# Three ring buffers instead of two for the halves of turned keys and queries, with separate counts for their transfers

## The chip, the cores and the metric

The kernel runs on one core of one Trainium2 chip. The metric is the device time of one execution in microseconds. Before the change three runs gave 3314.86, 3321.76 and 3323.79 us; the median is 3321.76 us.

## What is computed

The reference is one transformer layer, all in 32-bit floats, on x of shape (2, 2048, 256):

```python
q, k, v = x @ Wq, x @ Wk, x @ Wv              # 16 heads of 64
q, k = rmsnorm(q, q_rms_w), rmsnorm(k, k_rms_w)
gate = softplus(einsum("bthd,hd->bht", k, u_n) / 8)
bias = -max(i - j, 0) * omega_eff[h] * gate[b, h, i]
attn = softmax(causal(q @ k.T / 8 + bias))
x = layernorm(x + (attn @ v) @ Wproj)
h = silu(w1(x)) * w2(x); h = gelu(h1(h)); h = gelu(h2(h))
x = layernorm(x + w3(h))
```

## The kernel before, in words

The program has three stages on the same core: attention (to about 2170 us of the span), the first part of the feed-forward block, and the second. The change touches attention alone. To keep the precision of 32-bit floats with the matmul's rounded type, every operand is held as a rounded half ("hi") and a rest half ("lo").

Attention goes through 32 heads (2 batches of 16), in 16 pairs. One pair is projected at once (`project`, L984), its squares are made on POOL into `sq` (L637) and summed on DVE (L826). A head's score work consists of 40 units of 128 keys by up to 512 queries: PE makes the scores (L1027, L1028, and L1030 on the diagonal), ACT takes the exponential twice (rounded `e_hi` L716, full `e_all` L723), POOL makes the rest `e_lo` (L457), and PE multiplies by the values (L1045, L1050, L1052, L1061). Ahead of that, in a separate pass for the next head, PE makes the scores once in rounded form (`max`, L1008, two banks `ps_m`) and DVE takes their maxima (L907, L910), from which a shift row per block of queries comes.

The order of the work is one list written out by hand. `attention_steps` gives each extra step (load, project, turn, max, ...) a due time in units of heads and sorts them between the units of the head that is being scored. Every engine, and SP, which issues all transfers, walks the same list and takes the steps that concern it, so that each engine's queue is in the order of the list. A head n of a pair has its four turns near the end of the head before (even n) or shortly after the start of the head before it (odd n).

A turn (`turn`, n, qb; running number i = 4n + qb) is the step that the change is about. For 512 tokens:

- PE transposes keys and queries into a bank (L995), ACT copies the bank, scaled and rounded, into `kq_hi` (L700), DVE subtracts to get `kq_lo` (L896). Each of the two is a ring of two buffers, [128, 512].
- SP issues five transfers of 128 KB out of them, since the two halves of the 128 rows have to go to rows 0 to 63 of other tiles: `kq_hi` to `k_ext` (L506) and to `q_max` (L507), both counted by `hi_dup`; `kq_hi` to `k_split` (L511), counted by `lo_dup`; `kq_lo` to `k_split` (L513) and to `q_ext` (L514), counted by `lo_dup` too. In a head's first turn the transfer of its bias rows from DRAM (L510, `rows_in`) stands between L507 and L511.
- `turned` is the wait for `hi_dup`; PE takes it before the first `max` of each block of queries and before the first scores of a block, and SP before it doubles the queries (`twice`, L523). PE waits for `rows_in` before a head's first `max`. `lo_dup` is waited for before the first scores.

The waits before a buffer is overwritten are these (ACT, L696 to L699):

```python
if i >= 2:
    act.wait_ge(hi_dup[i % 2], 32 * (i // 2))
    act.wait_ge(lo_dup[i % 2], 48 * (i // 2))
    act.wait_ge(tr_free, i - 1)
```

So ACT may not copy turn i before all five transfers of turn i - 2 have landed, the last one (L514) among them, and the exponentials behind it on ACT's queue stand still.

Pair 8 begins the second batch, so x is turned anew between heads 14 and 15: eight transfers of 256 KB into the two `x_rows` tiles (L481), eight sets of transposes (L971).

Of the kernel before, what the change touches and what calls it, by code (L numbers as in the profile page):

```python
# [12 lines left out]
H, D = 16, 64  # L13
HID = 1024
P = 128
# [30 lines left out]
IDENT_MADE = 2  # L46
GP_CONSTANTS = 8 + H + 5 + 14
E_RING, HI_RING, LO_RING, Q_RING = 3, 4, 3, 3
HT = TT // 2
# [44 lines left out]
class Kept:  # L94
# [3 lines left out]
    def __init__(self, nc, ctx):  # L98
# [3 lines left out]
        def room(*uses):  # L102
# [16 lines left out]
        self.w3_hi, self.w3_lo, self.dn_x, self.dn_y = last  # L119
        (self.wp_in,), (self.silu, self.prod), (self.dn_gelu,), (self.sq,) = room(  # L120
            [("wp_in", [P, OC, C], F32)],
# [132 lines left out]
def attention(nc, x, wq, wk, wv, q_rms_w, k_rms_w, omega, u, yt_dram, recip_dram, rows_dram, kept, w1_w, w2_w, wproj):  # L254
    ctx = ExitStack()
    with ctx:
# [20 lines left out]
        v_full = [sb(f"v_full{i}", [P, NQB, TQ // 2, VCOLS]) for i in range(2)]  # L277
        x_rows = [sb(f"x_rows{i}", [P, 2, C]) for i in range(2)]
        k_split = [sb(f"k_split{i}", [P, T], F32R) for i in range(2)]
# [16 lines left out]
        bias_out = sb("bias_out", [P, P])  # L296
        kq_hi = [sb(f"kq_hi{i}", [P, QB], F32R) for i in range(2)]
        kq_lo = [sb(f"kq_lo{i}", [P, QB], F32R) for i in range(2)]
        maxes = sb("maxes", [P, TT, NQB])
# [55 lines left out]
        qk_hi = sem("qk_hi")  # L355
        hi_dup = [sem(f"hi_dup{i}") for i in range(2)]
        lo_dup = [sem(f"lo_dup{i}") for i in range(2)]
        rows_out = sem("rows_out")
# [40 lines left out]
        def turned(eng, n, qb):  # L399

            i = NTURN * n + qb
            eng.wait_ge(hi_dup[i % 2], 32 * (i // 2 + 1))

# [59 lines left out]
        def _(sp):  # L463
# [5 lines left out]
            for step in steps:  # L469
                if step[0] == "x in":  # L470
                    b, j = step[1:]
                    if b == 0:
                        rows = slice(j * T // 2, (j + 1) * T // 2)
# [27 lines left out]
                if step[0] == "turn":  # L501
                    n, qb = step[1:]
                    s, i = n % 2, NTURN * n + qb
                    cols = slice(qb * QB, (qb + 1) * QB)
                    sp.wait_ge(qk_hi, i + 1)
                    sp.dma_start(k_ext[s][0:D, cols].bitcast(F32), kq_hi[i % 2][0:D, :].bitcast(F32)).then_inc(hi_dup[i % 2], 16)  # L506
                    sp.dma_start(q_max[s][0:D, cols].bitcast(F32), kq_hi[i % 2][D:P, :].bitcast(F32)).then_inc(hi_dup[i % 2], 16)  # L507
                    if qb == 0:
                        sp.wait_ge(rows_out, 16 * (P // SQ) * (n // 2 + 1))
                        sp.dma_start(k_ext[s][R_BIAS:R_BIAS + NBIAS, :].bitcast(F32), rows_dram[:, s * TT:(s + 1) * TT, :, :].rearrange("c r a j -> c (r a j)")).then_inc(rows_in[s], 16)  # L510
                    sp.dma_start(k_split[s][0:D, cols].bitcast(F32), kq_hi[i % 2][0:D, :].bitcast(F32)).then_inc(lo_dup[i % 2], 16)  # L511
                    sp.wait_ge(tr_free, i + 1)
                    sp.dma_start(k_split[s][D:P, cols].bitcast(F32), kq_lo[i % 2][0:D, :].bitcast(F32)).then_inc(lo_dup[i % 2], 16)  # L513
                    sp.dma_start(q_ext[s][0:D, cols].bitcast(F32), kq_lo[i % 2][D:P, :].bitcast(F32)).then_inc(lo_dup[i % 2], 16)  # L514
                if step[0] == "twice":
# [58 lines left out]
        def _(gp):  # L574
# [42 lines left out]
            for step in steps:  # L617
# [11 lines left out]
                if step[0] == "square":  # L629
# [3 lines left out]
                    if p == 0 and i == 0:  # L633
                        gp.wait_ge(s_const, 1)
                    if p or i >= 4:
                        gp.wait_ge(ss_done, 8 * p + i - 3)
# [24 lines left out]
        def _(act):  # L661
# [6 lines left out]
            for step in steps:  # L668
# [23 lines left out]
                if step[0] == "turn":  # L692
                    n, qb = step[1:]
                    i = NTURN * n + qb
                    act.wait_ge(tr_full, i + 1)
                    if i >= 2:  # L696
                        act.wait_ge(hi_dup[i % 2], 32 * (i // 2))
                        act.wait_ge(lo_dup[i % 2], 48 * (i // 2))
                        act.wait_ge(tr_free, i - 1)  # L699
                    nc.scalar.activation(kq_hi[i % 2][:], work_bank(step)[:], ACT.Copy, scale=qk_w[:, 0:1]).then_inc(qk_hi, 1)  # L700
                if step[0] == "scores":
# [24 lines left out]
        def _(dve):  # L726
# [70 lines left out]
            for step in steps:  # L797
# [92 lines left out]
                if step[0] == "turn":  # L890
                    n, qb = step[1:]
                    i = NTURN * n + qb
                    dve.wait_ge(qk_hi, i + 1)
                    if i >= 2:
                        dve.wait_ge(lo_dup[i % 2], 48 * (i // 2))
                    nc.vector.scalar_tensor_tensor(kq_lo[i % 2][:], work_bank(step)[:], qk_w[:, 0:1], kq_hi[i % 2][:].bitcast(F32),  # L896
                                                   ALU.mult, ALU.subtract).then_inc(tr_free, 1)
# [51 lines left out]
        def _(pe):  # L949
            pe.wait_ge(s_cg, IDENT_MADE)  # L950

            for step in steps:
# [57 lines left out]
                if step[0] == "scores":  # L1010
# [6 lines left out]
                    if kt == 0:  # L1017
                        turned(pe, n, qb)
                        pe.wait_ge(lo_dup[grp % 2], 48 * (grp // 2 + 1))
                        pe.wait_ge(q_dup[grp % Q_RING], 32 * (grp // Q_RING + 1))  # L1020
                        pe.wait_ge(row_in[grp % 2], 16 * (P // SQ) * (grp // 2 + 1))
# [777 lines left out]
```

## Time and profile before

| | |
|---|---|
| runs | 3321.76, 3323.79, 3314.86 us |
| profiled execution, its own time | 3318.82 us |
| its span | 3317.0 us |
| mean granted clock of TensorE | 0.979 of full speed |
| PE busy | 3136.1 us, 95% of the span |
| ACT busy | 1792.3 us, 54% |
| DVE busy | 1669.2 us, 50% |
| POOL busy | 1491.5 us, 45% |

An engine's share is the union of its instructions' times over the span of 3317.0 us. SP executes no arithmetic: what counts for it is when each transfer is issued (rows of engine SPq), and a row's time there is how long the issue held the queue, not how long the data took. In the rows of a timeline the first column is the start in us from the span's start, the second the duration in us; `x4` means four instructions merged into one row; a bracket at the end gives how long the engine had been idle and what ended that.

### The profile page before, as it was taken

The numbers are of one execution on the slowest core, as the hardware profiler recorded it, in microseconds if no ns is written. First come the engines' busy times: TensorE is split into PE (matmuls) and PEld (weight loads), VectorE is DVE, ScalarE is ACT, GpSimd is POOL, SyncE is SP. The second block draws the span as 40 slices with busy tenths as digits, with TensorE's granted clock in tenths as the row PEclk, the third lists the DMA queues.
The fourth block names the chain that finished last, engine by engine and source line by source line (L and its number), as shares of the span: only waits on it lengthen the run. The fifth ranks groups of instructions, "written<-read, shape, count | busy, mean of one in ns | idle before, by whom it ended". The sixth has DMA issues, their size and how long they took to land. (4 is left out here: it accounts for less than half of the span.)

```text
span 3317.0 us, 45968 instructions
## 1 busy us (share of the span) xinstructions
PE 3136.1 (95%) x15472; PEld 2443.5 (74%) x15472; DVE 1669.2 (50%) x3928; ACT 1792.3 (54%) x3057; POOL 1491.5 (45%) x1306
## 2 busy tenths in 40 slices
PE   3899999999999999999999999989999999999998
PEld 3667767677677676676776776768888888788887
DVE  6566566565655665656556656463322222232323
ACT  1477677676766666666667766753333322322222
POOL 4476666666665666666667666621111110000000
PEclk7899999999999999999999999989999999999999
DMA  2332422422423224224233144432233333111110
GB/s 73 71 80 46 92 63 57 96 63 53 101 50 93 61 59 95 63 52 100 47 73 80 44 94 105 108 86 90 92 97 98 96 98 119 59 67 48 57 58 20
DMA packets 196523, 249.12 MB, mean 75 GB/s; under 512 B 67264, under 2 KB 95040, under 8 KB 196160
## 3 DMA queue, kind: packets, MB, share of 16 engines
q1 hardware_dynamic: 196288, 246.19, 28.9%
q8 instruction: 123, 2.02, 0.3%
q14 instruction: 112, 0.92, 0.1%
HBM read 84.86 MB, written 43.52 MB: 39 GB/s over the span
## 5 line engine op out<-in xcount | busy, mean ns | idle before, releaser
L457 POOL TENSOR_TENSOR e_lo<-e_all,e_hi 128x512 fp32r<-128x512 f32 (+1 forms) x832 | 1034.0, 1251 | 658.6 <-ACT e_all L723 590.9
L723 ACT ACTIVATE e_all<-ps_s,bias 128x512 f32<-128x512 f32 (+3 forms) x1280 | 787.4, 622 | 168.9 <-PE ps_s L1030 78.0
L910 DVE TENSOR_REDUCE maxes<-ps_m 128x1 f32<-128x512 f32 x768 | 521.3, 686 | 372.1 <-PE ps_m L1008 369.3
L716 ACT ACTIVATE e_hi<-ps_s,bias 128x512 fp32r<-128x512 f32 (+1 forms) x832 | 559.0, 672 | 228.4 <-PE ps_s L1028 133.0
L1008 PE MATMUL ps_m<-k_ext,q_max 128*128 128x512 f32 (+3 forms) x1280 | 462.7, 383 | 54.2 <-DVE maxes L910 25.0
L1027 PE MATMUL ps_s<-q_twice,k_split 128*128 128x512 f32 (+3 forms) x1280 | 477.7, 373 | 31.5 <-ACT e_all L723 26.5
L1028 PE MATMUL ps_s<-q_ext,k_ext 128*128 128x512 f32 (+3 forms) x1280 | 470.4, 368 | 0.0
L1061 PE MATMUL ps_v<-e_lo,v_main 128*66 128x512 f32 (+1 forms) x832 | 431.9, 519 | 17.2 <-POOL e_lo L457 17.2
L1008 PEld LDWEIGHTS ps_m<-k_ext,q_max 128*128 128x128 f32 x1280 | 245.7, 192 | 203.2 <-DVE maxes L910 60.2
L907 DVE CUSTOM_DVE_ANT_0 ps_m<-ps_m,mask_row 128x128 f32<-128x128 f32 (+3 forms) x512 | 252.6, 496 | 283.6 <-PE ps_m L1008 283.4
L1045 PE MATMUL ps_v<-e_all,v_full 128*66 128x512 f32 (+2 forms) x896 | 322.7, 442 | 0.0
L1050 PE MATMUL ps_v<-e_hi,v_main 128*66 128x512 f32 (+1 forms) x832 | 322.4, 387 | 0.0
L1052 PE MATMUL ps_v<-e_hi,v_rest 128*66 128x512 f32 (+1 forms) x832 | 320.9, 386 | 0.0
L1027 PEld LDWEIGHTS ps_s<-q_twice,k_split 128*128 128x128 f32 x1280 | 243.2, 190 | 99.2 <-issue 44.2
L1028 PEld LDWEIGHTS ps_s<-q_ext,k_ext 128*128 128x128 f32 x1280 | 243.2, 190 | 32.3
L1265 POOL TENSOR_TENSOR y_in<-y_in,r_in 128x512 f32<-128x512 f32 x56 | 75.2, 1343 | 377.1 <-DMA r_in<-recip_sums 377.1
L1642 ACT ACTIVATE dn_gelu<-dn_h,dn_scale 128x512 f32<-128x512 f32 x64 | 44.1, 689 | 321.9 <-PE dn_h L1740 321.9
L1611 POOL TENSOR_TENSOR dn_rs<-dn_rs,dn_power 128x4 f32<-128x4 f32 x8 | 8.1, 1007 | 462.2 <-DVE dn_rs L1702 462.2
L1061 PEld LDWEIGHTS ps_v<-e_lo,v_main 128*66 128x66 f32 x832 | 114.9, 138 | 126.1 <-issue 50.6
L1325 ACT ACTIVATE gelu<-up_h,up_scale 128x512 f32<-128x512 f32 x64 | 44.0, 688 | 296.7 <-PE up_h L1492 296.7
L1740 PE MATMUL dn_h<-a_lo,h_hi 128*128 128x512 f32 x512 | 204.3, 399 | 0.0
L1740 PE MATMUL dn_h<-a_hi,h_lo 128*128 128x512 f32 x512 | 204.1, 399 | 0.0
(245 smaller groups left out, 6074.6 us busy)
## 6 DMA issues: line engine op xcount, KB each, us to landing
q_twice<-q_max SPq DMA_DIRECT2D x256, 128.0 KB, 2.3
yt<-y_out SPq DMA_DIRECT2D x128, 130.0 KB
k_ext<-kq_hi SPq DMA_DIRECT2D x128, 128.0 KB, 2.3
q_max<-kq_hi SPq DMA_DIRECT2D x128, 128.0 KB, 2.4
k_split<-kq_hi SPq DMA_DIRECT2D x128, 128.0 KB, 2.4
k_split<-kq_lo SPq DMA_DIRECT2D x128, 128.0 KB, 2.4
q_ext<-kq_lo SPq DMA_DIRECT2D x128, 128.0 KB, 2.4
hidden<-gelu SPq DMA_DIRECT2D x64, 256.0 KB, 2.0
```

Source lines behind the costliest of these rows:

```text
L457: on.tensor_tensor(e_lo[:, i % LO_RING, off:QB], e_all[:, u_ % E_RING, off:QB], e_hi[:, i % HI_RING, off:QB].bitcast(F32), ALU.subtract).t ...
L716: nc.scalar.activation(e_hi[:, i % HI_RING, off:QB], ps_s[u_ % 2][:, off:QB], ACT.Exp, bias=by).then_inc(hi_done, 1)
L723: nc.scalar.activation(e_all[:, u_ % E_RING, off:QB], ps_s[u_ % 2][:, off:QB], ACT.Exp, bias=by).then_inc(ex_done, 1)
L910: nc.vector.tensor_reduce(maxes[:, qt, kc:kc + 1], ps_m[m % 2][:, 0:width], AX.X, ALU.max).then_inc(mx_free, 1)
L1008: nc.tensor.matmul(ps_m[m % 2][:, 0:width], q_max[s][:, qt * P:(qt + 1) * P], k_ext[s][:, kc * QB:kc * QB + width], start=True, stop=True) ...
L1027: nc.tensor.matmul(out, k_split[s][:, k], q_twice[grp % Q_RING][:, off:QB], start=True, stop=False)
L1028: last = nc.tensor.matmul(out, k_ext[s][:, k], q_ext[s][:, q], start=False, stop=not diag)
L1045: nc.tensor.matmul(bank[0:VCOLS, off:QB], v_full[s][:, kt // TQ, kt % TQ - TQ // 2, :], e_all[:, u_ % E_RING, off:QB], start=False, stop=k ...
L1050: nc.tensor.matmul(bank[0:VCOLS, off:QB], v_main[s][:, kt, :], e_hi[:, i % HI_RING, off:QB], start=kt == 0, stop=False, skip_group_check=True)
L1052: nc.tensor.matmul(bank[0:VCOLS, off:QB], v_rest[s][:, kt, :], e_hi[:, i % HI_RING, off:QB], start=False, stop=False, skip_group_check=Tru ...
L1061: nc.tensor.matmul(ps_v[(n * NQB + qb) % 2][0:VCOLS, off:QB], v_main[s][:, kt, :], e_lo[:, i % LO_RING, off:QB], start=False, stop=kt - TQ ...
L1740: last = nc.tensor.matmul(ps_h[o % 2][:], w[:, k, col], p[:, k, :], start=k == 0 and j == 0, stop=k == OC - 1 and j == 2)
```

## The change

- `kq_hi` and `kq_lo` become rings of three.
- The `kq_hi` to `k_split` transfer moves in SP's queue from behind the bias rows to before them, and is counted by `hi_dup`, which now goes up by 48 a turn; `lo_dup` goes up by 32.
- ACT waits for `hi_dup` and `tr_free` of turn i - 3 and no longer for `lo_dup`; DVE waits for `lo_dup` of turn i - 3. `turned` waits for three transfers.
- `x_rows` takes the room of `sq`, with a wait on SP before the first `x_rows` transfer of batch 1 (sums of pair 7 taken) and one on POOL before the first square of pair 8 (x turned).

```diff
+KQ_RING = 3
-        (self.wp_in,), (self.silu, self.prod), (self.dn_gelu,), (self.sq,) = room(
+        self.x_rows, (self.wp_in,), (self.silu, self.prod), (self.dn_gelu,), (self.sq,) = room(
+            [(f"x_rows{i}", [P, 2, C], F32) for i in range(2)],
...
-        x_rows = [sb(f"x_rows{i}", [P, 2, C]) for i in range(2)]
+        x_rows = kept.x_rows
...
-        kq_hi = [sb(f"kq_hi{i}", [P, QB], F32R) for i in range(2)]
-        kq_lo = [sb(f"kq_lo{i}", [P, QB], F32R) for i in range(2)]
+        kq_hi = [sb(f"kq_hi{i}", [P, QB], F32R) for i in range(KQ_RING)]
+        kq_lo = [sb(f"kq_lo{i}", [P, QB], F32R) for i in range(KQ_RING)]
...
         def turned(eng, n, qb):
             i = NTURN * n + qb
-            eng.wait_ge(hi_dup[i % 2], 32 * (i // 2 + 1))
+            eng.wait_ge(hi_dup[i % KQ_RING], 48 * (i // KQ_RING + 1))
...
                     b, j = step[1:]
+                    if b == 1 and j == 0:
+                        sp.wait_ge(ss_done, 8 * PAIRS // B)
...
                     sp.wait_ge(qk_hi, i + 1)
-                    sp.dma_start(k_ext..., kq_hi[i % 2][0:D, :]...).then_inc(hi_dup[i % 2], 16)
-                    sp.dma_start(q_max..., kq_hi[i % 2][D:P, :]...).then_inc(hi_dup[i % 2], 16)
+                    sp.dma_start(k_ext..., kq_hi[i % KQ_RING][0:D, :]...).then_inc(hi_dup[i % KQ_RING], 16)
+                    sp.dma_start(q_max..., kq_hi[i % KQ_RING][D:P, :]...).then_inc(hi_dup[i % KQ_RING], 16)
+                    sp.dma_start(k_split[s][0:D, cols]..., kq_hi[i % KQ_RING][0:D, :]...).then_inc(hi_dup[i % KQ_RING], 16)
                     if qb == 0:
                         sp.wait_ge(rows_out, 16 * (P // SQ) * (n // 2 + 1))
                         sp.dma_start(k_ext[s][R_BIAS:R_BIAS + NBIAS, :]..., rows_dram...).then_inc(rows_in[s], 16)
-                    sp.dma_start(k_split[s][0:D, cols]..., kq_hi[i % 2][0:D, :]...).then_inc(lo_dup[i % 2], 16)
                     sp.wait_ge(tr_free, i + 1)
...
+                    if p == PAIRS // B and i == 0:
+                        gp.wait_ge(xt_full, B * NXT)
...
-                    if i >= 2:
-                        act.wait_ge(hi_dup[i % 2], 32 * (i // 2))
-                        act.wait_ge(lo_dup[i % 2], 48 * (i // 2))
-                        act.wait_ge(tr_free, i - 1)
+                    if i >= KQ_RING:
+                        act.wait_ge(hi_dup[i % KQ_RING], 48 * (i // KQ_RING))
+                        act.wait_ge(tr_free, i - KQ_RING + 1)
...
-                    if i >= 2:
-                        dve.wait_ge(lo_dup[i % 2], 48 * (i // 2))
+                    if i >= KQ_RING:
+                        dve.wait_ge(lo_dup[i % KQ_RING], 32 * (i // KQ_RING))
...
-                        pe.wait_ge(lo_dup[grp % 2], 48 * (grp // 2 + 1))
+                        pe.wait_ge(lo_dup[grp % KQ_RING], 32 * (grp // KQ_RING + 1))
```

## Rows read from the trace of the kernel before

**Rows 1.** The page, busy time of the engines, in us.

```profile
PE   3136.1 (95%) x15472; PEld 2443.5 (74%) x15472; DVE 1669.2 (50%) x3928; ACT 1792.3 (54%) x3057; POOL 1491.5 (45%) x1306
```

**Rows 2.** PE's waits, 160 to 2170 us: total us, times, longest us.

```profile
PE ps_s L1027 <- ACT e_all L723: 26.5, 14, 2.7
...
PE ps_m L1008 <- issue: 13.8, 10, 2.1
PE ps_m L1008 <- DMA q_max<-kq_hi: 8.6, 8, 3.5
PE ps_t L971 <- DMA x_rows<-in_L_attn_x_dram: 3.3, 1, 3.3
```

**Rows 3.** Line L700, what ACT's idle time before it waited for: us, times.

```profile
  DMA q_ext<-kq_lo: 78.6, 33
```

**Rows 4.** Timeline, turns of head 16, all engines; the first two turns' transfers.

```profile
1121.90 0.60 SPq L507 DMA_DIRECT2D q_max<-kq_hi  x1
...
1122.55 0.48 SPq L510 DMA_DIRECT2D k_ext<-bias_rows  x1
...
1123.07 0.47 SPq L511 DMA_DIRECT2D k_split<-kq_hi  x1
...
1125.41 0.30 PE L1008 MATMUL ps_m<-k_ext,q_max 128*128 128x128 f32 x1 [1.40 <-issue]
...
1126.76 0.69 ACT L700 ACTIVATE kq_hi<-ps_t,qk_w 128x512 fp32r<-128x512 f32 x1 [1.79 <-DMA q_ext<-kq_lo]
...
1128.72 0.60 SPq L511 DMA_DIRECT2D k_split<-kq_hi  x1
...
1130.00 0.60 SPq L514 DMA_DIRECT2D q_ext<-kq_lo  x1
...
1130.71 0.39 PE L1008 MATMUL ps_m<-k_ext,q_max 128*128 128x512 f32 x1
```

**Rows 5.** The same timeline, fourth turn of head 16 and after it.

```profile
1129.28 0.60 PE L995 MATMUL ps_p<-ident,raw 128*128 128x128 f32 x4
...
1131.93 0.60 SPq L511 DMA_DIRECT2D k_split<-kq_hi  x1
...
1132.54 0.69 ACT L700 ACTIVATE kq_hi<-ps_p,qk_w 128x512 fp32r<-128x512 f32 x1 [3.00 <-DMA q_ext<-kq_lo]
...
1133.74 0.47 PE L1027 MATMUL ps_s<-q_twice,k_split 128*128 128x512 f32 x1 [1.93 <-ACT e_all L723]
```

**Rows 6.** Line L511, from issue to landing, 120 transfers, 160 to 2170 us.

```profile
DMA to landing us min/median/max: 2.3/2.4/5.5
```

**Rows 7.** Timeline of ACT, fourth turn of head 17, an odd one.

```profile
1171.88 0.69 ACT L700 ACTIVATE kq_hi<-ps_p,qk_w 128x512 fp32r<-128x512 f32 x1
```

**Rows 8.** Timeline of PE, third block of maxima of head 16.

```profile
1140.23 0.39 PE L1008 MATMUL ps_m<-k_ext,q_max 128*128 128x512 f32 x1
```

**Rows 9.** Timeline of the start, turns of head 0.

```profile
75.88 0.45 PE L1008 MATMUL ps_m<-k_ext,q_max 128*128 128x128 f32 x1 [4.71 <-DMA k_ext<-bias_rows]
...
83.81 0.75 DVE L896 SCALAR_TENSOR_TENSOR kq_lo<-ps_p,qk_w,kq_hi 128x512 fp32r<-128x512 f32 x1 [2.56 <-ACT kq_hi L700]
```

**Rows 10.** Timeline, x of the second batch, second set of transposes.

```profile
1000.18 0.59 SPq L481 DMA_DIRECT2D x_rows<-in_L_attn_x_dram  x1
...
1003.29 1.12 PE L971 MATMUL ps_t<-ident,x_rows 128*128 128x128 f32 x4 [3.31 <-DMA x_rows<-in_L_attn_x_dram]
```

**Rows 11.** Line L637, squares of pair 7, then of pair 8: duration ns, first and last start us.

```profile
L637 POOL TENSOR_TENSOR sq<-raw x8: 1037/1040/1043, 928.1 to 954.6; 128x512 f32<-128x512 f32 x8
...
L637 POOL TENSOR_TENSOR sq<-raw x8: 1032/1040/1043, 1068.1 to 1094.4; 128x512 f32<-128x512 f32 x8
```

**Rows 12.** Busy us (count) of PE, PEld, DVE, ACT, POOL, then clock, DMA share, GB/s.

```profile
603.40:606.80 3.40, 3.40 (x11) 2.73 (x10) 1.80 (x5) 2.08 (x4) 1.78 (x2) 0.50 0.39 87
...
856.00:859.40 3.40, 3.40 (x13) 2.73 (x12) 1.55 (x6) 1.95 (x3) 1.61 (x2) 0.50 0.67 163
...
1117.00:1134.00 17.00, 13.62 (x70) 9.50 (x70) 7.86 (x23) 11.31 (x21) 12.92 (x12) 1.00 0.62 141
```

More of the change, by code:

```diff
@@ L355, in attention @@
         qk_hi = sem("qk_hi")
-        hi_dup = [sem(f"hi_dup{i}") for i in range(2)]
-        lo_dup = [sem(f"lo_dup{i}") for i in range(2)]
+        hi_dup = [sem(f"hi_dup{i}") for i in range(KQ_RING)]
+        lo_dup = [sem(f"lo_dup{i}") for i in range(KQ_RING)]
         rows_out = sem("rows_out")
@@ L505, in _ @@
                     sp.wait_ge(qk_hi, i + 1)
-                    sp.dma_start(k_ext[s][0:D, cols].bitcast(F32), kq_hi[i % 2][0:D, :].bitcast(F32)).then_inc(hi_dup[i % 2], 16)
-                    sp.dma_start(q_max[s][0:D, cols].bitcast(F32), kq_hi[i % 2][D:P, :].bitcast(F32)).then_inc(hi_dup[i % 2], 16)
+                    sp.dma_start(k_ext[s][0:D, cols].bitcast(F32), kq_hi[i % KQ_RING][0:D, :].bitcast(F32)).then_inc(hi_dup[i % KQ_RING], 16)
+                    sp.dma_start(q_max[s][0:D, cols].bitcast(F32), kq_hi[i % KQ_RING][D:P, :].bitcast(F32)).then_inc(hi_dup[i % KQ_RING], 16)
+                    sp.dma_start(k_split[s][0:D, cols].bitcast(F32), kq_hi[i % KQ_RING][0:D, :].bitcast(F32)).then_inc(hi_dup[i % KQ_RING], 16)
                     if qb == 0:
@@ L510, in _ @@
                         sp.dma_start(k_ext[s][R_BIAS:R_BIAS + NBIAS, :].bitcast(F32), rows_dram[:, s * TT:(s + 1) * TT, :, :].rearrange("c r a j -> c (r a j)")).then_inc(rows_in[s], 16)
-                    sp.dma_start(k_split[s][0:D, cols].bitcast(F32), kq_hi[i % 2][0:D, :].bitcast(F32)).then_inc(lo_dup[i % 2], 16)
                     sp.wait_ge(tr_free, i + 1)
-                    sp.dma_start(k_split[s][D:P, cols].bitcast(F32), kq_lo[i % 2][0:D, :].bitcast(F32)).then_inc(lo_dup[i % 2], 16)
-                    sp.dma_start(q_ext[s][0:D, cols].bitcast(F32), kq_lo[i % 2][D:P, :].bitcast(F32)).then_inc(lo_dup[i % 2], 16)
+                    sp.dma_start(k_split[s][D:P, cols].bitcast(F32), kq_lo[i % KQ_RING][0:D, :].bitcast(F32)).then_inc(lo_dup[i % KQ_RING], 16)
+                    sp.dma_start(q_ext[s][0:D, cols].bitcast(F32), kq_lo[i % KQ_RING][D:P, :].bitcast(F32)).then_inc(lo_dup[i % KQ_RING], 16)
                 if step[0] == "twice":
@@ L695, in _ @@
                     act.wait_ge(tr_full, i + 1)
-                    if i >= 2:
-                        act.wait_ge(hi_dup[i % 2], 32 * (i // 2))
-                        act.wait_ge(lo_dup[i % 2], 48 * (i // 2))
-                        act.wait_ge(tr_free, i - 1)
-                    nc.scalar.activation(kq_hi[i % 2][:], work_bank(step)[:], ACT.Copy, scale=qk_w[:, 0:1]).then_inc(qk_hi, 1)
+                    if i >= KQ_RING:
+                        act.wait_ge(hi_dup[i % KQ_RING], 48 * (i // KQ_RING))
+                        act.wait_ge(tr_free, i - KQ_RING + 1)
+                    nc.scalar.activation(kq_hi[i % KQ_RING][:], work_bank(step)[:], ACT.Copy, scale=qk_w[:, 0:1]).then_inc(qk_hi, 1)
                 if step[0] == "scores":
@@ L893, in _ @@
                     dve.wait_ge(qk_hi, i + 1)
-                    if i >= 2:
-                        dve.wait_ge(lo_dup[i % 2], 48 * (i // 2))
-                    nc.vector.scalar_tensor_tensor(kq_lo[i % 2][:], work_bank(step)[:], qk_w[:, 0:1], kq_hi[i % 2][:].bitcast(F32),
+                    if i >= KQ_RING:
+                        dve.wait_ge(lo_dup[i % KQ_RING], 32 * (i // KQ_RING))
+                    nc.vector.scalar_tensor_tensor(kq_lo[i % KQ_RING][:], work_bank(step)[:], qk_w[:, 0:1], kq_hi[i % KQ_RING][:].bitcast(F32),
                                                    ALU.mult, ALU.subtract).then_inc(tr_free, 1)
```

## The prediction

> **What bounds the kernel now.** I read the page first. TensorE is busy for 3136.1 of 3317.0 us [rows 1]; the other engines are near half. So nothing that shortens ACT, DVE or POOL work counts by itself; what counts is where PE stands still in attention, the only stage that the diff touches. PE's own waits between 160 and 2170 us are the second view [rows 2]. The largest entry, 26.5 us in 14 waits, is PE waiting with the scores for an ACT exponential. Then come two entries for a head's or a block's first maxima (13.8 us in 10, where the page names no releaser, and 8.6 us in 8), and 3.3 us once for x.
>
> The third view tells why ACT is late: before its copy of a turn (L700) it stands idle for 78.6 us in 33 cases until the transfer `q_ext<-kq_lo` has landed [rows 3]. That is `lo_dup` of turn i - 2. The timeline of head 16 shows both ends. The second turn's last transfer is issued at 1130.00, ACT's copy of the fourth turn starts at 1132.54 after 3.00 us of idleness, and PE's next scores start at 1133.74 after 1.93 us [rows 4, 5]. The third turn's copy waits 1.79 us too, but PE loses nothing behind it: its maxima at 1130.71 start on time. In the odd head 17 the same copy starts without a wait [rows 7]. So the stall is one for each even head, in its fourth turn: 14 of them.
>
> SP is the pacemaker behind this. In one even head's phase its issues stand back to back, each holding the queue for 0.47 to 0.60 us [rows 4, 5], so the second turn's transfers are out seven microseconds after the copy.
>
> **The change, part by part.**
>
> *Third buffer, lo_dup no longer in ACT's wait.* ACT now waits for the rounded half's three transfers of turn i - 3. For the fourth turn that is the first turn, whose transfers are issued by 1123.07 and land 2.4 us later (5.5 at the worst) [rows 4, 6], while PE's transposes of the fourth turn end at 1129.88 (start 1129.28 and 0.60) [rows 5]. ACT will not wait. DVE's wait is for turn i - 3's rest, also landed. All 14 PE waits go: minus 26.5 us. One of them is given back. In head 14 the second set of x transposes waits for a transfer that SP issues at 1000.18; PE starts at 1003.29 after 3.31 us [rows 10]. SP's queue there is full and doesn't move, so PE only waits longer. I put this stall at 1.9 us (the mean, 26.5 / 14). Term: minus 24.6 us. What is late next after a removed stall: the maxima of the third block, which need the third turn's transfers. Their last is issued at 1131.93 and lands by 1134.3; PE is there at 1140.23 [rows 5, 6, 8], two microseconds sooner after the change, so covered by 3.8 us.
>
> *The start.* Head 0 has no scores beside it and PE follows DVE. DVE's subtraction in the fourth turn waits 2.56 us for ACT [rows 9]. Bounds are 0 and 2.56; I take 2.1, since ACT's copy of 0.69 us still lies between bank and DVE. Term: minus 2.1 us.
>
> *k_split ahead of the bias rows.* PE's first maxima of an even head wait for the bias rows. In head 0 the profile names them [rows 9]; in head 16 the rows are issued at 1122.55 and PE starts at 1125.41, while `q_max`, issued at 1121.90, is in at 1124.3 [rows 4, 6]. PE had stood still for 1.40 us. The moved transfer holds the queue for 0.47 us where it was, and 0.60 us plus 0.04 between rows when it follows another transfer out of `kq_hi` [rows 4, 5]. So the bias rows leave 0.47 to 0.64 us later; I take 0.64, the pitch in the place it moves to. Even heads except 14, where the x wait swallows it, are 15: plus 9.6 us. The rest of SP's order is the same number of issues, so nothing later on the queue moves.
>
> *turned counts three.* The second block's maxima (1130.71) then need the second turn's `k_split`, issued at 1128.72, in at 1131.1 [rows 4, 6]. By then PE is itself 0.64 us later, 1131.35: the two delays overlap. Nothing added, 0.3 us a head at most. In odd heads first maxima come long after the rows; nothing.
>
> *x_rows in the squares' room.* The last square of pair 7 starts at 954.6 and the first of pair 8 at 1068.1 [rows 11]; the x transfers and transposes lie between (from about 994 to 1036). Both new waits are met before they are reached: 0 us. They stand at the head of SP's and POOL's queues, so were one not met, everything behind it would wait; the cover is 35 us at either end. The tiles' new addresses: 0.
>
> *TensorE's clock.* After some of these waits the granted clock reads 0.50, the 1.2 GHz level, for 3.4 us, as at 603.4 and 856.0 [rows 12]. Three further such stretches (1265.6, 1395.3, 1528.4) read alike. Four of the five follow a fourth-turn wait, the one at 856.0 a first-maxima wait. Work in it takes double, so one costs 1.7 us. The four go: minus 6.8 us. But first-maxima waits grow from 1 to 2 us up to 1.6 to 2.7 us, and I put two new stretches on them: plus 3.4 us. Term: minus 3.4 us; bounds minus 8.5 and plus 17.
>
> Sum: -24.6 - 2.1 + 9.6 - 3.4 = -20.5 us, on the profiled execution's own 3318.82 us: 3298.3. That execution lies 2.9 us under the median of the runs shown, so against the median it is **3301 us**.
>
> The row says that the queue is held for 0.60 us by a transfer that lands after 2.4 us, a quarter of it [rows 4, 6]. The Trainium skill (DMA: Bandwidth & Descriptors, "Issuing engines are not separate DMA queues") says that the time a sequencer takes to initiate a DMA is usually small relative to the DMA itself. By that rule the moved transfer would cost nothing and the sum would be 30.1 us instead of 20.5. The trace disagrees, and I go by it.
>
> **The rivals.**
>
> *The queue paces PE (slower).* If PE at the second and third block of an even head has to wait for SP anyway, the removed stall comes back there, and the delays of rows and third transfer add instead of overlapping: 15 x (0.64 + 0.64) = plus 19 us, 3341. It decides at the third block: PE at 1140.23 less 2 us against 1134.3. For it: SP's issues are back to back. Against it: that margin.
>
> *The clock (no change).* If every lengthened first-maxima wait is followed by a half-clock stretch, 15 x 1.7 = 25.5 us come in and the five old ones (8.5) go: -24.6 - 2.1 + 9.6 + 17 = -0.1 us, 3322. For it: 856.0. Against it: most waits of this size have none behind them, five stretches for some 30 waits of 1 to 2.8 us. The Trainium skill (TensorE: Matmul & The Clock Gate, "Why this matters for your kernels") asks that idle gaps between bursts be avoided since they bring the low clock back; it speaks against lengthening any wait.
>
> *POOL refills half.* In the 17 us around head 16's turns POOL is busy for 12.92 [rows 12]; two microseconds less raise it from 76% to 86%. If it takes back half of what ACT gives, 12.3 us are lost again: 3313.5.
>
> **How the numbers follow.** My own case 0.78, the clock 0.10, POOL 0.07, the queue 0.05. The own case's bounds: best -24.6 - 2.6 + 7.2 (0.48 x 15) - 8.5 = -28.5 and 2 us of matmul tails, about 3291; worst, two or three more slow stretches and 0.3 us a head at the second block, about 3311. The range of 0.8 reaches 3289 to 3315. A measurement of this kernel can tell 0.3%, 10 us, from no change. Below 3311.8: my case, 0.78. Within 0.3%: clock and POOL, 0.17. Above: the queue, 0.05.
>
> **What would show it.** ACT's idle time before L700 for `q_ext<-kq_lo` gone; PE's entry for scores waiting on ACT down from 26.5 to a few us; PE's first-maxima waits up by 0.6 us each; the x wait near 1000 longer than 3.31; fewer 0.50 readings. It would be wrong if PE's waits at L1008 rise by over 15 us, or if PE waits for POOL where it waited for ACT.

## The result, and the profile after

The changed kernel takes 3307.8 us (median of 10 runs, 3302.93 to 3312.4) against 3321.12 us for the kernel before (10 runs, 3314.86 to 3325.47): a ratio of 0.9963, 95% interval 0.9953 to 0.9972, or about 13 us less. The forecast was 3301 us and 20.5 us less. The direction and the removed stall are right, the size is not: the two profiled executions (3318.82 and 3302.93 us) lie 15.9 us apart where the sum said 20.5. The start of the page after:

```profile
span 3301.1 us, 45840 instructions
...
PE 3133.5 (95%) x15472; PEld 2444.2 (74%) x15472; DVE 1669.9 (51%) x3928; ACT 1799.5 (55%) x3057; POOL 1492.5 (45%) x1306
```

Busy time has moved little on any engine [rows 1]. PE was idle for 180.9 us of its span before and for 167.6 now, so 13.3 us of the span's 15.9 are idle time and 2.6 are busy time. PE's waits of the changed kernel, 160 to 2170 us (total us, times, longest us):

```profile
PE ps_m L1013 <- issue: 28.5, 13, 3.2
...
PE ps_m L1013 <- DMA k_split<-kq_hi: 6.9, 4, 4.6
...
PE ps_t L976 <- DMA x_rows<-in_L_attn_x_dram: 3.4, 1, 3.4
PE ps_p L976 <- DMA x_rows<-in_L_attn_x_dram: 2.0, 1, 2.0
```

The entry for scores waiting on an ACT exponential, 26.5 us before [rows 2], is gone: no wait of that kind is left. The maxima (now L1013) stand still for 28.5 + 6.9 = 35.4 us where it was 13.8 + 8.6 = 22.4, so 13.0 us came back there. All but 0.5 us of the 35.4 (0.9 of the 22.4) lie ahead of the first maxima of the 15 even heads from 2 to 30. The x transfers of the second batch cost 5.4 us; before it was 3.3 and another 0.5 on the first set. ACT's copy (now L705) names what its idle time waited for, to be read against [rows 3]:

```profile
its engine sat idle before it (us, times) until:
  PE ps_t L1000: 36.0, 17
  PE ps_p L1000: 28.0, 17
```

The copy waits for PE's transposes alone and for no landing. The timeline of head 16, whose bias rows are now issued 4.6 us earlier, shows the trade in one place:

```profile
1116.68 0.60 SPq L511 DMA_DIRECT2D q_max<-kq_hi  x1
...
1117.32 0.59 SPq L512 DMA_DIRECT2D k_split<-kq_hi  x1
...
1117.96 0.48 SPq L515 DMA_DIRECT2D k_ext<-bias_rows  x1
...
1121.22 0.30 PE L1013 MATMUL ps_m<-k_ext,q_max 128*128 128x128 f32 x1 [2.71 <-issue]
...
1125.68 0.69 ACT L705 ACTIVATE kq_hi<-ps_p,qk_w 128x512 fp32r<-128x512 f32 x1 [0.70 <-PE ps_p L1000]
```

The bias rows leave 1.28 us behind `q_max` instead of 0.65 [rows 4], and PE starts 3.26 us after their issue instead of 2.86, so PE stands 2.71 us instead of 1.40. In return the fourth turn's copy no longer waits 3.00 us [rows 5]. In head 0 a line of the start and in batch 1 a line of the x stage answer to [rows 9, 10]; both are in the timeline:

```profile
77.69 0.45 PE L1013 MATMUL ps_m<-k_ext,q_max 128*128 128x128 f32 x1 [5.53 <-DMA k_ext<-bias_rows]
...
83.38 0.75 DVE L901 SCALAR_TENSOR_TENSOR kq_lo<-ps_p,qk_w,kq_hi 128x512 fp32r<-128x512 f32 x1 [0.38 <-ACT kq_hi L705]
...
997.79 1.11 PE L976 MATMUL ps_t<-ident,x_rows 128*128 128x128 f32 x4 [3.38 <-DMA x_rows<-in_L_attn_x_dram]
```

Summed up by windows from the end of head 0's start to the first maxima of head 30, first before (111 to 2041 us), then after (110 to 2026 us); columns as in [rows 12]:

```profile
111.00:2041.00 1930.00, 1840.38 (x9052) 1375.73 (x9051) 1168.35 (x2922) 1332.76 (x2322) 1264.42 (x1091) 0.99 0.31 71
```

```profile
110.00:2026.00 1916.00, 1838.30 (x9054) 1376.69 (x9051) 1169.38 (x2923) 1339.79 (x2324) 1267.18 (x1091) 0.99 0.31 72
```

Idle time of PE fell from 89.6 to 77.7 us, by 11.9, which is what the wait entries give (26.5 - 13.0 - 1.6). Busy time fell by 2.1 us, 1.0 us had been saved up to the end of head 0's start, and 0.9 us was saved behind these windows: 15.9.

**The clock.** Between 150 and 2160 us the granted clock read 0.50 for 27.3 us before, in six stretches of 3.4 us and one of 6.8, and for 30.7 us after, in seven of 3.4 and one of 6.8. Before, four followed a fourth-turn wait; now none does. Of the changed kernel's eight, six begin in the last 0.7 us of a first-maxima wait of an even head or up to 1.1 us behind it, one in the x wait, and the long one (2024.6) in head 30's wait of 4.6 us. The long one before (2040.4) stood in head 30's wait too. So seven of the 15 first-maxima waits have a stretch, where two had one. The length of the wait alone doesn't decide: those of head 12 (3.16 us) and head 16 (2.71 us) have none, that of head 22 (1.94 us) has one. Behind attention it evens out: from 150 us to the end the two executions stand at half clock for 54.6 us each. One of the six in the timeline of PE:

```profile
587.26 0.40 PE L1033 MATMUL ps_s<-q_ext,k_ext 128*128 128x512 f32 x1
587.50 0.40 PE L1055 MATMUL ps_v<-e_hi,v_main 128*66 128x512 f32 x1
...
590.58 0.30 PE L1013 MATMUL ps_m<-k_ext,q_max 128*128 128x128 f32 x1 [2.45 <-issue]
...
592.36 0.63 PE L1055 MATMUL ps_v<-e_hi,v_main 128*66 128x512 f32 x1
```

After 2.45 us of idleness a 512-column matmul of L1055 takes 0.63 instead of 0.40 us. Two such matmuls start 0.24 us apart ahead of the gap. The window of 3.4 us from 591.0 on has a clock of 0.52, near the 1.2 GHz level, and the next one of 5.6 us has 0.98 (columns as in [rows 12]):

```profile
591.00:594.40 3.40, 3.40 (x14) 2.73 (x12) 1.61 (x6) 1.95 (x3) 1.15 (x2) 0.52 0.76 171
594.40:600.00 5.60, 5.60 (x32) 4.13 (x31) 3.12 (x11) 3.42 (x7) 1.90 (x2) 0.98 0.81 180
```

### The profile page after: what moved, and what is told of

It is laid out like the page before. It is cut to its first block and busy times, and to the rows that moved or that the text cites. A ratio compares the mean times of both kernels' runs of the same rounds, so it can differ in the third digit from the quotient of the medians.

```text
span 3301.1 us, 45840 instructions
## 1 busy us (share of the span) xinstructions
PE 3133.5 (95%) x15472; PEld 2444.2 (74%) x15472; DVE 1669.9 (51%) x3928; ACT 1799.5 (55%) x3057; POOL 1492.5 (45%) x1306
## 5 line engine op out<-in xcount | busy, mean ns | idle before, releaser
L1013 PE MATMUL ps_m<-k_ext,q_max 128*128 128x512 f32 (+3 forms) x1280 | 462.4, 382 | 66.0 <-issue 28.5
L1066 PE MATMUL ps_v<-e_lo,v_main 128*66 128x512 f32 (+1 forms) x832 | 430.9, 518 | 17.2 <-POOL e_lo L459 17.2
L1013 PEld LDWEIGHTS ps_m<-k_ext,q_max 128*128 128x128 f32 x1280 | 245.4, 192 | 214.8 <-issue 76.9
L1055 PE MATMUL ps_v<-e_hi,v_main 128*66 128x512 f32 (+1 forms) x832 | 323.2, 388 | 0.0
```

Source lines behind the costliest of these rows:

```text
L1013: nc.tensor.matmul(ps_m[m % 2][:, 0:width], q_max[s][:, qt * P:(qt + 1) * P], k_ext[s][:, kc * QB:kc * QB + width], start=True, stop=True) ...
L1055: nc.tensor.matmul(bank[0:VCOLS, off:QB], v_main[s][:, kt, :], e_hi[:, i % HI_RING, off:QB], start=kt == 0, stop=False, skip_group_check=True)
L1066: nc.tensor.matmul(ps_v[(n * NQB + qb) % 2][0:VCOLS, off:QB], v_main[s][:, kt, :], e_lo[:, i % LO_RING, off:QB], start=False, stop=kt - TQ ...
```

## The experiments

Each kernel ran 4 to 11 times beside the kernel before, whose medians were 3320.3 us (beside e1 to e4), 3321.3 (e5, e6, e8, e9) and 3320.7 (e7, e10 to e12). A ratio is to that kernel, with its 95% interval.

| kernel | median us | ratio | PE idle at maxima, us |
|---|---|---|---|
| before | 3321.1 | 1 | 22.4 |
| changed | 3307.8 | 0.9963 [0.9953, 0.9972] | 35.4 |
| e1_rows_first | 3296.5 | 0.9933 [0.9921, 0.9946] | 28.5 |
| e2_move_only | 3318.9 | 1.0000 [0.9991, 1.0009] | 34.3 |
| e3_ring_only | 3286.0 | 0.9902 [0.9888, 0.9916] | 24.3 |
| e4_two_buffers | 3308.4 | 0.9966 [0.9952, 0.9979] | 35.1 |
| e5_rows_second | 3284.8 | 0.9891 [0.9869, 0.9912] | 20.3 |
| e6_rows_last | 3337.7 | 1.0051 [1.0032, 1.0069] | 53.7 |
| e7_x_rows_only | 3320.9 | 1.0004 [0.9995, 1.0013] | 23.9 |
| e8_ring_and_move | 3305.5 | 0.9955 [0.9940, 0.9969] | 36.5 |
| e9_two_rows_first | 3304.8 | 0.9951 [0.9933, 0.9969] | 29.1 |
| e10_filler | 3288.0 | 0.9904 [0.9890, 0.9917] | 9.9 |
| e11_ring_filler | 3280.3 | 0.9886 [0.9871, 0.9901] | 8.3 |
| e12_rows_second_filler | 3282.4 | 0.9887 [0.9873, 0.9900] | 9.2 |

The last column adds the entries of PE's waits at the maxima that name no releaser ("<- issue") or a DMA, between 160 and 2170 us. Most of it lies ahead of a head's first maxima; a few waits at the second block of queries are in it too.

Some parts below are told by "lengths": 3.4 us at half clock is one length, and a stretch of 6.8 us is two. They are counted from 150 us up to the stretch at head 30's first maxima: eight before and nine in the changed kernel.

### The order of SP's queue: e1, e6 and e2

e1_rows_first is the changed kernel with `k_split` back behind the bias rows, its count unchanged:

```diff
                     sp.dma_start(q_max[s]...).then_inc(hi_dup[i % KQ_RING], 16)
-                    sp.dma_start(k_split[s][0:D, cols]..., kq_hi...).then_inc(hi_dup[i % KQ_RING], 16)
                     if qb == 0:
                         ...
+                    sp.dma_start(k_split[s][0:D, cols]..., kq_hi...).then_inc(hi_dup[i % KQ_RING], 16)
```

> The changed kernel with the k_split transfer back behind the bias rows; rings of three and the count of three in hi_dup stay. Theory A (the move of the transfer costs: the bias rows leave 0.64 us later and land some 0.25 us later, so PE's first maxima in 15 even heads wait 0.9 us longer, 13 us in all): the 13 us come back but for 0.1 us a head, since the first maxima now need k_split, which lands about with the bias rows; 3295 to 3299 us against 3308 for the changed kernel, PE's idle time at L1013 without a DMA as releaser down from 28.5 us to about 15. Rival B (it is the count of three in turned that lengthens the first maxima's wait): no better than the changed kernel, 3306 to 3310 us.

Measured 3296.5 us, 11.3 us less than the changed kernel. PE's waits:

```profile
PE ps_m L1013 <- DMA k_split<-kq_hi: 28.5, 21, 4.0
```

The time is within theory A's 3295 to 3299 us. Its waits are not: PE stands still for 28.5 us, not for about 15. The rows are early again, but the maxima now wait for `k_split`, which is the last of the three that `turned` counts. Of the 28.5 us 24.6 are ahead of the first maxima and 3.9, in six waits, at the second block, where the prediction had put nothing.

e6_rows_last moves the bias rows further back, behind all five transfers of the turn:

```diff
                     sp.dma_start(k_split[s][0:D, cols]..., kq_hi...).then_inc(hi_dup[i % KQ_RING], 16)
-                    if qb == 0:
-                        ...
                     sp.wait_ge(tr_free, i + 1)
                     ...
                     sp.dma_start(q_ext[s][0:D, cols]..., kq_lo...).then_inc(lo_dup[i % KQ_RING], 16)
+                    if qb == 0:
+                        ...
```

> The changed kernel with the bias rows behind all five transfers of the turn, two issues of 0.60 us later than in the changed kernel. Theory A: first maxima of 15 even heads 1.2 us later, with more half-clock stretches behind them: plus 18 to 27 us, 3326 to 3335 us against 3308. Rival B (the count of three, not the bias rows, sets the start): 3306 to 3312.

Measured 3337.7 us, 29.9 us above the changed kernel, slower than before and 3 us above theory A's range. PE's waits:

```profile
PE ps_m L1013 <- issue: 53.7, 15, 5.1
```

The entry grew by 18.3 us against 35.4, that is 1.2 us a head, two issues of 0.47 to 0.60 us. The time grew by 30, so the order has a price beyond the idle microseconds. The pages of the two profiled executions, 33.6 us apart in span, divide it: PE's idle time grew by 18.5 us (167.6 to 186.1) and its busy time, with the same matmuls, by 15.1 us (3133.5 to 3148.6). The half-clock lengths went from nine to 18.

e2_move_only is the kernel before with nothing but that move, its two buffers and counts left as they were:

```diff
                     sp.dma_start(q_max[s]...).then_inc(hi_dup[i % 2], 16)
+                    sp.dma_start(k_split[s][0:D, cols]..., kq_hi...).then_inc(lo_dup[i % 2], 16)
                     if qb == 0:
                         ...
-                    sp.dma_start(k_split[s][0:D, cols]..., kq_hi...).then_inc(lo_dup[i % 2], 16)
```

> The kernel before with the k_split transfer put ahead of the bias rows and nothing else; rings of two, old counts. Theory A: the stall of the fourth turn stays (PE's scores wait on ACT about 26 us) and the first maxima of even heads wait 0.9 us longer: plus 11 to 15 us, 3332 to 3336 us against 3321. Rival B: the order of two issues is worth nothing by itself, 3319 to 3323 us.

Measured 3318.9 us: no change, as rival B had it and against theory A. PE's waits say why:

```profile
PE ps_m L1008 <- issue: 34.3, 15, 4.4
...
PE ps_s L1027 <- ACT e_all L723: 11.6, 9, 2.0
```

The first-maxima waits grew by 11.9 us, as in the changed kernel, and the fourth turn's stall shrank by 14.9 us, from 26.5 to 11.6. ACT's idle time on `q_ext` fell with it, from 78.6 [rows 3] to 41.9 us. Two buffers make the fourth turn wait for a transfer that SP's queue issues on its own schedule. PE comes 0.8 us a head later (11.9 / 15) and waits 1.1 us a head less there (14.9 / 14). The stall absorbs a delay as long as it exists.

### The third buffer: e3, e8, e4 and e9

e3_ring_only has three buffers and x's rows in the squares' room, but the order and the counts of before; ACT waits for both counts of turn i - 3:

```diff
...
-                    if i >= 2:
-                        act.wait_ge(hi_dup[i % 2], 32 * (i // 2))
-                        act.wait_ge(lo_dup[i % 2], 48 * (i // 2))
-                        act.wait_ge(tr_free, i - 1)
+                    if i >= KQ_RING:
+                        act.wait_ge(hi_dup[i % KQ_RING], 32 * (i // KQ_RING))
+                        act.wait_ge(lo_dup[i % KQ_RING], 48 * (i // KQ_RING))
+                        act.wait_ge(tr_free, i - KQ_RING + 1)
...
```

> Rings of three with the order and the counts of the kernel before (k_split behind the bias rows and in lo_dup; ACT waits for hi_dup and lo_dup of turn i - 3). Theory A: the third buffer alone removes the fourth turn's stall, separate counting adds nothing to it, and nothing is paid: minus 25 to 27 us against the kernel before, 3294 to 3297 us; ACT idle for a landing before L705 under 3 us. Rival C (what removes the stall is that lo_dup is no longer in ACT's wait): ACT still waits and the time lies above 3310 us.

Measured 3286.0 us, 34 us below the kernel before that ran beside it and 22 below the changed kernel. Theory A was right in kind, but its 3294 to 3297 us were 8 us too high. PE's waits:

```profile
PE ps_m L1014 <- issue: 20.5, 13, 3.7
...
PE ps_m L1014 <- DMA q_max<-kq_hi: 3.8, 5, 1.2
```

There is no stall of the scores, and the maxima wait 24.3 us, about what they did before. Beside the idle time the clock gained: four half-clock lengths are left of eight. So neither separate counts nor the new order is needed to remove the stall.

e8_ring_and_move puts the move, and only the move, on top of e3:

```diff
                     sp.dma_start(q_max[s]...).then_inc(hi_dup[i % KQ_RING], 16)
+                    sp.dma_start(k_split[s][0:D, cols]..., kq_hi...).then_inc(lo_dup[i % KQ_RING], 16)
                     if qb == 0:
                         ...
-                    sp.dma_start(k_split[s][0:D, cols]..., kq_hi...).then_inc(lo_dup[i % KQ_RING], 16)
```

> The ring-only kernel (three buffers, old counts) plus the move of the k_split transfer ahead of the bias rows. The move alone was free beside rings of two. Theory A' (it was free there because the fourth turn's stall, whose end SP's queue sets, took up the delay; without the stall it is paid in full): 3296 to 3300 us against 3286. Rival (the move is free everywhere and the changed kernel pays for the count of three alone): 3284 to 3288.

Measured 3305.5 us: the move costs 19.5 us here, more than theory A' gave it, and costs nothing beside two buffers (e2). PE's waits:

```profile
PE ps_m L1014 <- issue: 36.2, 15, 4.5
```

With 0.3 us at `q_max` that is 12.2 us more idle time than in e3. The other 7 us are not in PE's waits. The clock is the likely cause: the profiled execution of e8 was the slowest of its eight (3313.24 us), and in it PE's busy time is 14.6 us longer than in e3's (3141.8 to 3127.2), with 13 half-clock lengths instead of four. The filler runs below bear on it. Its 3305.5 us and the changed kernel's 3307.8 are alike: with three buffers and this order it makes no difference how the transfers are counted.

e4_two_buffers is the changed kernel with `KQ_RING = 2`, so separate counts and the new order on two buffers:

```diff
-KQ_RING = 3
+KQ_RING = 2
```

> The changed kernel with rings of two: only the separate counting and the move are left. Theory A: ACT's fourth turn copy waits for the second turn's k_split (about 1.2 us instead of 3.0), DVE's subtraction for the second turn's last transfer as before, so part of the stall comes back through DVE and the banks of maxima: 3314 to 3322 us. Rival C (the counting alone removes the stall, the third buffer does nothing): 3306 to 3310 us, like the changed kernel.

Measured 3308.4 us, the same as the changed kernel. The expectation missed. In the changed order, with the counts apart, the third buffer is worth nothing. It differs from e2_move_only in the counts (and in x's rows, worth 0 by e7), so with two buffers the separate counts are worth 10.5 us. In line L705 the copy waits for no landing:

```profile
its engine sat idle before it (us, times) until:
  PE ps_t L1000: 36.4, 16
  PE ps_p L1000: 28.5, 16
  issue: 3.7, 2
```

e9_two_rows_first takes the third buffer from e1 in the same way:

```diff
-KQ_RING = 3
+KQ_RING = 2
```

> Count of three and rows first as in e1_rows_first, but rings of two. With the move in place rings of two and of three took the same time. Theory D (the late bias rows hid what the second buffer's missing third costs; with rows first ACT and DVE reach the fourth turn before the second turn's transfers have landed): 3300 to 3308 us against 3296 for three buffers. Rival C (counting apart is all that was needed, the third buffer is worth nothing): 3295 to 3298.

Measured 3304.8 us against e1's 3296.5: with the rows first, the third buffer is worth 8.3 us. DVE's waits, which have no such entry with three:

```profile
DVE kq_lo L901 <- DMA q_ext<-kq_lo: 19.9, 11, 2.7
```

DVE's subtraction waits until a `kq_lo` buffer has been read. In e4 the same entry is 4.9 us in 5 waits, where PE stands 35.1 us at the maxima instead of 29.1. I read it as the pattern of e2: where PE comes later anyway, the second buffer is free in time. How these waits reach PE is not shown, as PE's own named waits are only 1 us longer in e9 than in e1.

### Where else the rows could stand, and x's rows: e5 and e7

e5_rows_second is e3 with the bias rows ahead of `q_max` too:

```diff
                     sp.dma_start(k_ext[s][0:D, cols]...).then_inc(hi_dup[i % KQ_RING], 16)
-                    sp.dma_start(q_max[s]...).then_inc(hi_dup[i % KQ_RING], 16)
                     if qb == 0:
                         ...
+                    sp.dma_start(q_max[s]...).then_inc(hi_dup[i % KQ_RING], 16)
```

> Rings of three with the old counts as in the ring-only kernel, and the bias rows issued straight behind k_ext, ahead of q_max. Theory A (PE's first maxima of an even head start when the bias rows land, and these leave 0.6 us earlier): 0.5 us less in each of 15 even heads and one or two half-clock stretches fewer, 3275 to 3280 us against 3286. Rival (q_max, pushed back by one issue, now lands last and binds): gain under 3 us, 3283 to 3287.

Measured 3284.8 us, within the interval of e3 and where the rival had it. PE's waits:

```profile
PE ps_m L1014 <- DMA q_max<-kq_hi: 20.3, 19, 3.0
```

`q_max` takes the place of the rows as what lands last. Each of the two is needed, so exchanging them gains only the difference of their landings.

e7_x_rows_only is the kernel before with x's rows in the squares' room and the two waits that this needs:

```diff
...
+                    if b == 1 and j == 0:
+                        sp.wait_ge(ss_done, 8 * PAIRS // B)
...
+                    if p == PAIRS // B and i == 0:
+                        gp.wait_ge(xt_full, B * NXT)
```

> The kernel before with nothing but x_rows in the squares' room and the two waits that go with it. All theories: both waits are met tens of us before they are reached, 0 us, 3318 to 3323. If the new waits or addresses cost something, SP's or POOL's queue shows a wait near 994 or 1068 us.

Measured 3320.9 us, ratio 1.0004: 0 us, as forecast. This part only makes room.

### What PE's idle time costs beyond itself: e10, e11 and e12

Here PE does work that nobody reads while it would stand still ahead of the first maxima of each even head from 2 on. The bank is one that the maxima are about to overwrite, and nothing of the computation is left out. e10_filler puts six such matmuls into the changed kernel:

```diff
+                    if v == 0 and n % 2 == 0 and n:
+                        pe.wait_ge(mx_free, m - 1)
+                        for _ in range(6):
+                            nc.tensor.matmul(ps_m[m % 2][:], ident_r[:], k_ext[1 - s][:, 0:QB], start=True, stop=True)
```

> The changed kernel with six matmuls of 512 columns that nobody reads, put on PE ahead of the first maxima of each even head but the first; they take 1.4 us of a wait of 1.7 to 3.3 us and change no wait. Theory E (a good part of what the move costs is the half-clock stretches behind these waits, eight or nine of 1.7 us each): the 0.50 readings near first maxima go and 10 to 14 us come back, 3294 to 3298 us against 3308. Rival F (the waits themselves are the whole cost, the clock readings are the same with fewer idle us): 3305 to 3310.

Measured 3288.0 us: 19.8 us less than the changed kernel, with 90 matmuls more. Windows of 30 us of the changed kernel that each contain one of its half-clock stretches:

```profile
450.00:480.00 30.00, 27.79 (x125) 19.10 (x125) 17.29 (x46) 21.72 (x37) 21.65 (x18) 0.94 0.60 133
580.00:610.00 30.00, 27.51 (x125) 19.14 (x124) 16.99 (x46) 21.73 (x36) 21.37 (x18) 0.94 0.59 132
...
1240.00:1270.00 30.00, 27.00 (x124) 18.80 (x123) 16.81 (x44) 21.17 (x36) 21.16 (x18) 0.94 0.59 131
```

The same windows of e10:

```profile
450.00:480.00 30.00, 29.18 (x137) 20.04 (x136) 17.61 (x46) 23.11 (x39) 21.90 (x19) 1.00 0.59 133
580.00:610.00 30.00, 29.43 (x138) 20.44 (x137) 17.39 (x44) 22.68 (x38) 22.01 (x19) 1.00 0.59 132
...
1240.00:1270.00 30.00, 29.62 (x142) 20.83 (x141) 19.07 (x49) 20.65 (x34) 19.53 (x18) 1.00 0.46 102
```

The clock reads 1.00 in these windows. Two half-clock lengths are left, one in the x wait and one in head 30's wait, where the changed kernel has nine. The waits:

```profile
PE ps_m L1017 <- issue: 6.4, 14, 0.8
...
PE ps_m L1017 <- DMA k_split<-kq_hi: 3.5, 1, 3.5
```

The waits shrank by 25.5 us, and 90 fillers at 0.24 us (the pitch of two 512-column matmuls above) fill 22 of these, so some 4 us of waiting vanished as well. Seven lengths less, at 1.7 us each as the prediction priced them, are 12 us; at the end of attention one came in (6.8 us instead of 3.4), which leaves 10. Together 14 us, against 15.3 between the two profiled executions. The two pages agree: PE's idle time fell by 26.6 us (167.6 to 141.0) and its busy time grew by 11.3 (3133.5 to 3144.8), which is 21.6 for the fillers less 10.2 for six lengths. The medians lie 19.8 us apart, since the profiled execution of the changed kernel was the fastest of its ten. Why the rows come earlier with respect to PE was not traced. The expectation, 10 to 14 us back, was too low.

e11_ring_filler puts four of them into e3, whose waits are shorter:

```diff
+                        for _ in range(4):
```

> The ring-only kernel (3286 us) with four such matmuls. Its trace has only two or three half-clock stretches between 160 and 2160 us that follow first maxima. Theory E: 2 to 5 us come back, 3281 to 3284. Rival F: 3285 to 3288.

Measured 3280.3 us (3278.47 to 3285.71), 5.7 us below e3 and 40.8 us below the kernel before: the lowest median of all. Its interval still touches e3's, so the gain over e3 is likely, not certain; theory E had 2 to 5 us.

e12_rows_second_filler puts three into e5.

```diff
+                        for _ in range(3):
```

> The kernel with the bias rows second (3285 us) and three such matmuls. One half-clock stretch to gain at most: 3281 to 3285 us, by either theory within 3 us of the kernel without them; the test is whether it beats the ring-only kernel.

Measured 3282.4 us, within the expected range. The interval and that of e11 overlap almost wholly, so the place of the rows ahead of or behind `q_max` is again of no account.

## Why the prediction was right in direction and too large in size

**The stall, right.** All 14 waits are gone, 26.5 us, and ACT waits for no landing. What was given back at x is 1.6 us; 1.9 were forecast. The prediction's reading of SP was loose: it has the second turn's transfers out seven microseconds after the copy, but the trace has ten (copy at 1120.42, last issue at 1130.00 and 0.60), and its cover of 3.8 us at the third block is 3.9.

**The third buffer as the cause, wrong.** The prediction argued that the stall goes because turn i - 3 has long landed. That is a sufficient cause (e3), but in the changed kernel it isn't the one that acts. e4 shows the same time with two buffers: there ACT's wait is gone because it no longer counts the rest half's transfers. Two causes stood ready, either enough with this order, and the prediction named them in one heading without asking what each was worth alone.

**k_split ahead of the bias rows, mis-sized.** Forecast was 0.64 us in 15 heads, 9.6 us. Measured: 13.0 us of idle time at the maxima of 15 heads, 0.9 a head (head 14 is among them, which the prediction left out, and head 0, which it counted, has another 0.8). The order itself is as forecast (1.28 against 0.65 us). The rest is in what follows it: in head 16 PE starts 3.26 us after the rows' issue instead of 2.86 [rows 4]. Over the 14 even heads from 2 to 28 the median of this time went from 2.93 to 3.18 us. The prediction took this time as unmoved; why it grew is open.

**Terms that don't add.** The sum charged the move against the state before. There it costs nothing (e2), for the stall took it in; once the stall is gone, it costs 19.5 us (e8 against e3). The right reading was: the third buffer alone is worth 34 to 35 us, and the move takes 20 of them back. The sum priced the move at 9.6.

**The clock, the wrong sign in its count.** Forecast: four stretches go and two come, minus 3.4 us. Measured up to 2160 us: four went and five came, 27.3 to 30.7 us at half clock. PE's busy time still fell by 2.1 us, so this execution doesn't show the term as a loss of 1.7; but e10 shows that the stretches hang on these waits. So the step "I put two new stretches on them" failed, and the rival that priced all 15 first-maxima waits at a stretch each was too strong: seven of 15 have one. The list of five that both started from was short too: the trace of before has another stretch at 1002.8, in the x wait, and the long one at 2040.4. The price of 1.7 us each holds: e3 and e4 run the same matmuls, and from 150 us to the very end e4's profiled execution has 24 lengths and 3148.0 us of busy PE where e3's has 12 and 3127.2, so 20.8 / 12 = 1.7 us a length. The Trainium skill (TensorE: Matmul & The Clock Gate, "Why this matters for your kernels") asks that idle gaps between bursts be avoided; the runs agree, with the size beside it: with 25.5 us of these waits gone through unread matmuls the kernel took 19.8 us less, some 10 of them by the clock.

**The issue time, right.** The Trainium skill (DMA: Bandwidth & Descriptors, "Issuing engines are not separate DMA queues") calls the time to initiate a DMA usually small relative to the DMA. By that rule e1, e6 and e8 would not have moved. They moved by 11, 30 and 19.5 us for one or two issues ahead of the bias rows, and 0.47 to 0.60 us of a landing of 2.4 us is no small part. The measurement decides.

**turned counts three, right here only.** In the changed order it adds nothing (the changed kernel and e8 differ by 2.3 us, with overlapping ranges). With the rows first it costs 10.5 us (e1 against e3): PE's maxima then wait for a transfer that they don't read, 2.2 us longer in the first block and 2.1 in the second. The rest of the 10.5 is not in PE's waits; there are seven half-clock lengths against four, some 5 us.

**The start, right.** DVE's wait fell from 2.56 to 0.38 us, by 2.2 where 2.1 was forecast. PE's wait ahead of the first maxima grew by 0.8 (5.53 against 4.71 [rows 9]), which is the move's price in head 0. The net of 1.4 us is what the stage shows: ACT's first copy starts at 71.24 instead of 70.25, the first scores at 105.40 instead of 105.84. The 1.0 us ahead of it lies where the diff touches nothing. Another 0.6 us was saved right behind, as the half-clock stretch of the start ended near 110 us instead of 112.

**x_rows and the rivals.** x_rows cost 0 (e7). At the second block PE waits for SP twice, 0.5 us in all, and at the third never, so the queue rival falls; POOL's entry is 17.2 us in 14 waits in both kernels, so that rival falls too.

**Open.** Where half-clock stretches fall differs from one execution to the next: the profiled executions of e4 and e8 (3317.4 and 3313.24 us) were the longest of all their executions and held 15 and 13 lengths. So a count from one profile can be off by several. Of e3's 34.0 us between the spans 25.1 are PE's idle time, 22.4 of them in its named waits (52.7 to 30.3: scores, maxima and x), and 8.9 are busy time, of which four lengths less make 6.8. Nor was it tried to bring the bias rows on another queue, which would separate their issue from the turns' transfers.

One rival to the third buffer stands untested. ACT's copy of the fourth turn waited for the second turn's transfers. Between these and the first turn's, SP issues five transfers of weights, which hold its queue for 2.7 us; so it does in heads 2, 8, 16, 18 and 28 alike. In head 16 of the kernel before:

```profile
1120.42 0.69 ACT L700 ACTIVATE kq_hi<-ps_p,qk_w 128x512 fp32r<-128x512 f32 x1
...
1124.87 0.59 SPq L487 DMA_DIRECT2D w_in<-in_L_attn_Wv_dram  x1
...
1127.05 0.47 SPq L491 DMA_DIRECT2D w_in<-in_L_attn_Wq_dram  x1
```

PE lost 1.9 us a head there. No run moves these transfers behind the turns, so how much of the stall that alone would have removed is not known.

## What to carry to other kernels

A wait whose end is set by another queue absorbs every delay ahead of it. Price a second edit against the state without that wait, as the parts don't add: here the move cost 0 us before and 20 us after. In a full issue queue the place of one transfer that the busiest engine needs next can be worth more than half of what a deeper ring is (20 us against 35 here). Put ahead of everything else what it needs, and let it wait for nothing that it doesn't read. Where PE must stand still for 2 to 3 us again and again, unread matmuls in the gap can pay for themselves: they gave 20 us beside 35 us of such waits, and 6 or 2 us, hardly outside the noise, beside 24 and 20 us. Shortening the wait is better where it can be done, as e3 without fillers matches e10 with them.

## What the runs showed of the hardware

TensorE's granted clock fell to 0.50 for 3.4 or 6.8 us at or shortly behind single idle times of 1.9 to 4.6 us amid otherwise dense work (changed kernel), but only at some of them: 3.16 us had none. With the gaps filled it stayed at 1.00 there (e10), worth some 10 us of 3308. Each 3.4 us at half clock cost 1.7 us of PE's time (e4 against e3). An issue of 0.60 us on SP ahead of a needed transfer delayed its reader by 0.9 us on average, more than the issue itself, since the time from issue to the reader's start grew too (median 2.93 to 3.18 us).
